# Four pairs' one-hots in two comparisons instead of eight: a graph network's relation stage on one core

## The reference

```python
# SAGE, twice: mean over incoming edges
agg = segment_sum(x[src], dst, n) / max(deg, 1)
out = agg @ Wl.T + bl + x @ Wr.T
# relational layer, three times: one mean per destination and relation
seg = dst * 5 + etype
agg = segment_sum(x[src], seg, n * 5) / cnt          # 0 where cnt is 0
out = einsum('nrd,rdk->nk', agg.reshape(n, 5, -1), W) + x @ root + bias
# whole
x = layernorm(x + sage2(relu(sage1(x))))
h = concat(x, node_emb[node_type])                   # 256 wide
x = layernorm(x + relu(rgcn3(relu(rgcn2(relu(rgcn1(h)))))))
```

## Time and profile before

| | |
|---|---|
| median of three runs | 5596.16 us (5591.11 to 5609.0) |
| the profiled execution: its own time | 5605.28 us |
| its span | 5603.4 us |
| mean granted TensorE clock | 0.89 |

### The profile page before, as it was taken

How to read it: one execution, slowest core, us unless ns; L and a number is a source line. 1 busy time by engine, 2 the same in 40 slices (tenths; PEclk the granted TensorE clock), 3 DMA queues, 4 the chain that set the end, 5 groups by cost and what they waited for, 6 DMA issues and landing times.

```text
span 5603.4 us, 86440 instructions
## 1 busy us (share of the span) xinstructions
PE 4453.9 (79%) x30196; PEld 3138.0 (56%) x30196; DVE 2632.7 (47%) x7852; ACT 3177.9 (57%) x4502; POOL 3190.0 (57%) x3114
## 2 busy tenths in 40 slices
PE   2688999996666666666566666599999979999998
PEld 1466666663344334434343434477777757777776
DVE  5888882113656666566666666212222221222222
ACT  2566661002444444444444444399888978888887
POOL 5000000004777777777777777477777746777775
PEclk7799999997777878788887888799999989999999
DMA  3223324654555656565555556567776766666664
GB/s 96 87 113 143 121 113 157 241 217 128 145 168 145 175 146 173 142 174 152 160 166 147 169 146 173 186 224 259 255 262 219 260 228 204 207 212 207 212 208 157
DMA packets 629486, 994.44 MB, mean 177 GB/s; under 512 B 359122, under 2 KB 511324, under 8 KB 625212
## 3 DMA queue, kind: packets, MB, share of 16 engines
q1 hardware_dynamic: 159412, 552.80, 27.7%
q0 software_dynamic: 146944, 302.80, 19.0%
q10 hardware_dynamic: 322696, 133.28, 8.8%
HBM read 715.99 MB, written 272.14 MB: 176 GB/s over the span
## 4 chain that ended last, share of the span: by engine, by line
PE 37%; POOL 23%; issue 8%; DVE 4%; DMA 3%; ACT 1%; SPq 1%; ACTq 0%; DVEq 0%; POOLq 0%
PE couple_bank L1530 27%; POOL messages L1481 23%; PE bank L1496 5%; DMA slices<-relations_d 1%; DMA messages<-table,src_rows 1%; PE bank L1568 1%; SPq L1401 1%; DVE ring L1839 1%; PE bank L1554 1%; DVE scaled L1832 1%; DVE type_scaled L1832 1%; DMA type_scaled<-node_hot 1%; PE bank L1544 1%; PE couple_bank L1512 1%; ACT lots L1318 0%
## 5 line engine op out<-in xcount | busy, mean ns | idle before, releaser
L1481 POOL DMA_INDIRECT messages<-table,src_rows x2320 | 2415.9, 1041 | 820.7 <-issue 652.9
L1318 ACT CAST lots<-slices 128x1024 fp32r<-128x1024 fp8e4 (+1 forms) x1750 | 1674.4, 1027 | 260.2 <-PE couple_bank L1530 216.1
L1530 PE MATMUL couple_bank<-lots,pieces 128*128 128x512 f32 x6860 | 1715.6, 403 | 16.5 <-ACT lots L1318 16.3
L1647 ACT CAST stage<-couple_bank 128x980 fp8e4<-128x980 f32 x896 | 841.0, 985 | 1132.1 <-PE couple_bank L1512 978.4
L1530 PEld LDWEIGHTS couple_bank<-lots,pieces 128*128 128x128 f32 x6860 | 1256.7, 189 | 325.9 <-ACT lots L1318 57.4
L1496 PE MATMUL bank<-group_hot,messages 128*128 128x120 bf16 x9084 | 692.4, 234 | 399.4 <-DMA messages<-table,src_rows 359.1
L1496 PEld LDWEIGHTS bank<-group_hot,messages 128*128 128x128 bf16 x9084 | 584.5, 107 | 662.6 <-issue 615.6
L1481 POOL DMA_INDIRECT messages<-table,rel_rows x708 | 688.7, 973 | 326.3 <-issue 173.6
L1793 DVE TENSOR_TENSOR ring<-ring,bank 128x120 f32 x354 | 99.1, 280 | 1464.8 <-PE bank L1496 1461.4
L1512 PE MATMUL couple_bank<-rel_hot,lo_dense_hot 128*128 128x490 bf16 x1792 | 597.6, 446 | 196.1 <-ACT stage L1647 178.3
L1462 POOL IOTA iota_rel_i<- 128x120 int32 (+1 forms) x4 | 1.7, 469 | 1185.7 <-DMA table<-typed_rows 1185.7
(11 more groups left out here) (272 smaller groups left out, 3851.2 us busy)
## 6 DMA issues: line engine op xcount, KB each, us to landing
slices<-relations_d SPq DMA_DIRECT2D x210, 768.0 KB
relations_d<-stage ACTq DMA_DIRECT2D x336, 240.0 KB
adjacency_d<-adjacency SPq DMA_DIRECT2D x15, 4704.0 KB, 14.5
adjacency<-adjacency_d SPq DMA_DIRECT2D x15, 4704.0 KB, 15.3
slices<-relations_d SPq DMA_DIRECT2D x70, 832.0 KB
pieces<-dense SPq DMA_DIRECT2D x42, 896.0 KB, 11.0
messages<-table,src_rows POOLq DMA_INDIRECT x2320
dense<-table_halves SPq DMA_DIRECT2D x49, 640.0 KB
```

The lines of the kernel that those rows point to most:

```text
L1318: return copy(to, of_slice[:, :, first:end, :])
L1481: pool.indirect_dma_start(messages_in(i)[:, t, 0:ROWS[v]], None, GATHERED[v], bass.IndirectOffsetOnAxis(ap=rows[:, e:e + 1], axis=0)).then ...
L1530: mm = pe.matmul(bank[DENSE_BANKS[K % 2]][:, 0:DENSE_COLS], pieces[M % PIECE_RING][:, tile % PIECE_TILES, half * P:(half + 1) * P], lots[l ...
L1647: act.copy(to, from_banks, saturate=False).then_inc(rel_evicted, 1)
```

## The change

Both loops over the four pairs of a batch go; one `tensor_tensor` comparison makes the four low one-hots (512 elements in each partition) and one the four relation one-hots (1960 elements). The iota is repeated over the pairs by a broadcast of the middle dimension, and each code over the columns by a broadcast of the last. Buffers, values, the wait and the signal stay.

```diff
             def dense_onehots(b):
                 if b >= HOT_RING:
                     vec.wait_ge(rel_psum, (b - HOT_RING + 1) * BATCH // 2)
-                for m in range(BATCH):
-
-                    vec.tensor_scalar(lo_dense_hot[:, b % HOT_RING, m, :], iota16[:, :], lo_dense[:, b * BATCH + m:b * BATCH + m + 1], None, ALU.is_equal)
-                    op = vec.tensor_scalar(rel_hot[:, b % HOT_RING, m, :], iota_rel[:, :], rel_dense[:, b * BATCH + m:b * BATCH + m + 1], None, ALU.is_equal)
-                op.then_inc(rel_hot_made, 1)
+                codes = slice(b * BATCH, (b + 1) * BATCH)
+                vec.tensor_tensor(lo_dense_hot[:, b % HOT_RING, :, :], iota16[:, :].unsqueeze(1).broadcast_to([P, BATCH, P]),
+                                  lo_dense[:, codes].unsqueeze(2).broadcast_to([P, BATCH, P]), ALU.is_equal)
+                vec.tensor_tensor(rel_hot[:, b % HOT_RING, :, :], iota_rel[:, :].unsqueeze(1).broadcast_to([P, BATCH, REL_COLS]),
+                                  rel_dense[:, codes].unsqueeze(2).broadcast_to([P, BATCH, REL_COLS]), ALU.is_equal).then_inc(rel_hot_made, 1)
```

## The result

The changed kernel takes 6087.58 us, the median of four runs (6082.78 to 6094.56), against 5599.93 us for the kernel before in its four runs: 1.0865 times as long, with a 95% interval of 1.0852 to 1.0878. The forecast was 6278 us with a range of 6010 to 6485 us. The profiled execution took 6084.78 us.

What follows compares the result with a forecast made beforehand. The prediction took POOL's gather issues to bound the first relational layer: 448 batches x 1.7 us of hold (+762) less 80 given back is +682 us on 5605.3, hence 6287, or 6278 us for the median; range 6010 to 6485 us.

Steps and rivals of the forecast that it cites:

- What bounds the stage: First relational layer: POOL issues gathers without a pause, 1596 issues of 1.066 + 0.305 us making the stage's 2188 us.
- The new instructions' durations: VectorE's two comparisons in each batch: 0.68 us for 512 elements and 2.19 us for 1960, 2.87 us busy.
- POOL is held for the whole instruction: A POOL issue begun under a VectorE product of two SBUF tensors waits for its end: 1.7 us a batch, +762 us.
- low end of 1.1 us: Lowest hold of POOL a batch, if it asks as the batch begins and next turns late: +413 us, 6009 us.
- The pair of scalings: Two VectorE products, 4.83 us together, cost POOL 3.32 us; that ratio gave 1.9 us for a batch.
- Given back: Part of POOL's 169 us excess in the first relational layer that goes with the old tensor_scalars: 80 us.
- VectorE's extra occupation costs nothing: First relational layer: +147 us busy and +497 us occupation, covered by VectorE's 786 us of waiting for TensorE.
- R5: Rival: VectorE becomes the bound as well, or holds run on into group_hot; above 6484 us, chance 0.04.
- R1: Rival: the new comparisons do not hold POOL, which loses its 80 us of excess; 5516 us, chance 0.06.
- R2: Rival: VectorE's comparisons stream slower, 1.77 ns an element, 4.7 us a batch; about 7000 us, chance 0.06.
- R3: Rival: POOL keeps in step with the batches, hold only 0.2 to 1.0 us; 5620 to 5970 us, chance 0.07.
- R4: Rival: no change in time, because the six slots hide POOL's delay; chance 0.02.

Runs made afterwards that it cites:

- e4: The changed kernel with codes stored twice in f16 and both comparisons written over pairs of elements: 5711.55 us, +108 us against the kernel before.
- e12: The kernel before with two memsets, clearing both one-hot buffers, ahead of each batch's eight scalar comparisons: 5790.41 us, +190 us against the kernel before.
- e2: The changed kernel with one low and one relation two-tensor comparison for each pair, eight a batch: 6032.79 us, +429 us against the kernel before.
- e5: The changed kernel with the relation comparison cut in four, one for each pair, the low one kept whole: 5938.41 us, +328 us against the kernel before.

## Why the prediction was right, and where it was off

- **What bounds the stage** (POOL's issues without a pause): right. From its first gather to its last the stage grew by 482 us, and POOL's busy time in it by the same.
- **The new instructions' durations:** right to 8 ns. 683 and 2187 ns were worked out from other two-tensor rows, 685 and 2195 ns measured. The elements cost four times what they did, and the six saved instructions did not make up for it: 1.04 ns an element against 0.27, so the count of instructions was the wrong thing to save. The Trainium skill (VectorE: DVE Perf Modes, "Rules for kernel authors") advises to keep the number of instructions low. The Trainium skill also gives a 16-bit `tensor_scalar` twice the rate of the best two-tensor form (VectorE: DVE Perf Modes, "The perf-mode tier table"). The trace agrees for e4's form (1171 - 420 ns for 1448 elements, 0.52 ns each, against 0.27). The change's form, whose codes are f32, ran at half of e4's rate.
- **POOL is held for the whole instruction:** right in mechanism, and the price is the term that was mis-sized. The text took 1.7 us a batch, between 1.5 (POOL always slips in between the two comparisons) and 2.16 (never). Measured: 1.23 + 0.09, or 1.31 us before rounding, 588 us in place of 762. An issue held by the low comparison got in at its end, and at each of the 448 ends of the relation comparison one got in, so slipping in was the case to take. The rest, from 1.48 down to 1.31, is that issues do not begin at even odds over the batch: many begin 1.22 us into the relation comparison. The measured price lies below that of slipping in, and the range holds it only through its low end of 1.1 us, which the text described (POOL asks as the batch begins, its next turn falls late) but could not price from rows. The pair of scalings, from which I took the ratio of 1.9 us, is the row where slipping in fails at times, and it was the wrong nearest row for a short instruction ahead of a long one.
- **Given back:** 80 us were taken; measured 104, since 65 of the 169 us of excess stay with the scalings and the other operations. 588 - 104 = 484, and the time grew by 488.
- **VectorE's extra occupation costs nothing:** right in the changed kernel, but partly by luck. e12 shows that 583 us of occupation alone cost 190 us, so the argument "63% busy, therefore covered" does not hold. The prediction's +147 us of busy time was wrong as well: it took the old rows' 1138.8 us, which overlap each other, as time of VectorE. The page shows +430.7 us, and VectorE at 1778.55 of 2660 us, where R5 counted 1498 of 2860. This makes rival R1 wrong as it was priced: had the comparisons not held POOL, VectorE's occupation would probably have eaten the 80 us, by the measure of e12's 190 for a larger dose; 5516 us was too low by this estimate.
- **R2** (a slower stream) fell with the 2195 ns, **R3** (phases lower the hold) was right in kind for 0.17 us a batch (its own prices of 0.2 to 1.0 us give 5606 to 5964 us, not 5620 to 5970), **R4** fell with TensorE's 777.8 us, and **R5** does not show.

## What to carry to other kernels

When GpSimd issues indirect DMAs without a pause, the price of a VectorE instruction with two SBUF inputs is how long it holds the next issue, not its own time: if issues began evenly over it, one of length L, longer than the issue's period T, would cost about L - T / 2. That is an estimate, and it came out high here: 1.56 us for the relation comparison, against 1.23 measured behind a shorter instruction. The same operation with an input in PSUM held nothing in this kernel. Before eight scalar comparisons become one of two tensors, read the rate for each element from rows of both kinds, and see which engine's queue is without a gap. And "covered, because the engine is 63% busy" wants an experiment that occupies the engine and holds nothing, as e12 does.

## What was not expected of the hardware

- A memset holds no issue: of 253 that began inside one of e12's 0.88 us memsets none took over 0.97 us. The Trainium skill (SBUF — State Buffer, "SBUF: two separate sides") names only two SBUF inputs and the two-port modes as what locks the ports against GpSimd, and the trace agrees. By the same section of the Trainium skill, two SBUF inputs lock only against a GpSimd instruction that reads SBUF, a condition that the prediction left out. Every gather here takes its row numbers (`src_rows`, `rel_rows`) from SBUF, so the condition may well be met; no run here has an issue without such an input.
- The end of an instruction does not always let POOL in. From a scalar comparison to the group one-hot that follows at once it mostly doesn't (in the kernel before 67 issues that began ahead of a group one-hot were held to its end, 36 us in all; 4 got in at the comparison's end); from the long two-tensor comparison to the next instruction it always did (448 of 448); in rows of 0.28 and 0.66 us two-tensor instructions an issue is at times passed over until the row ends, with issues of 3.3 us and, at most, 6.6 us in e2 and 7.6 us in e5. The rule of the Trainium skill, of a lock for one whole instruction, does not contain this.
